# Attention with a group norm in front: the first transferred group sends 12 of its 16 squares, GpSimd copies the other four, and the homes are three

## The reference

```python
y = ((xg - mu) * rsqrt(var + EPS)).reshape(B, C, H, W) * gn_gamma + gn_beta   # 4 groups of 32 channels
q, k, v = split(einsum('bchw,dc->bdhw', y, w_qkv) + b_qkv, 3)
scores = einsum('bnc,bcm->bnm', q, k) * C ** (-0.5)
w = softmax(scores, axis=-1)
a = einsum('bnm,bmc->bnc', w, v)
out = einsum('bchw,dc->bdhw', a, w_out) + b_out
return x + out
```

## Time and profile before

| what | us |
|---|---|
| median of three runs | 137.77 |
| lowest and highest run | 137.07, 138.37 |
| profiled execution, its own time | 138.07 |
| its span, first to last instruction | 136.3 |
| PE busy | 129.4 (95% of the span) |
| DVE busy | 99.8 (73%) |
| ACT busy | 65.0 (48%) |
| POOL busy | 41.4 (30%) |

### The profile page before, as it was taken

How to read it: one execution, slowest core, us unless ns; L and a number is a source line. 1 busy time by engine, 2 the same in 40 slices (tenths; PEclk the granted TensorE clock), 3 DMA queues, 4 the chain that set the end, 5 groups by cost and what they waited for, 6 DMA issues and landing times.

```text
span 136.3 us, 1759 instructions
## 1 busy us (share of the span) xinstructions
PE 129.4 (95%) x543; PEld 89.1 (65%) x543; DVE 99.8 (73%) x170; ACT 65.0 (48%) x117; POOL 41.4 (30%) x49
## 2 busy tenths in 40 slices
PE   6999999998999949999999999999999999999990
PEld 6987688875777526666666666666656577554670
DVE  0589699999998996877686889866868886761302
ACT  3154778854675372544542475544633474730000
POOL 6032130730022229300190058000770367303210
PEclk9999999999999999999999999999999999999999
DMA  4940000030056978985689656888888459961011
GB/s 152 350 191 0 0 5 0 3 77 0 0 111 147 210 188 236 207 203 169 154 204 206 204 114 160 191 195 224 203 202 201 122 123 209 209 176 77 0 77 77
DMA packets 8937, 19.01 MB, mean 139 GB/s; under 512 B 3040, under 2 KB 3040, under 8 KB 8928
## 3 DMA queue, kind: packets, MB, share of 16 engines
q1 hardware_dynamic: 8640, 18.63, 53.8%
q10 hardware_dynamic: 288, 0.27, 0.6%
HBM read 4.20 MB, written 2.11 MB: 46 GB/s over the span
## 4 chain that ended last, share of the span: by engine, by line
PE 75%; DVE 12%; SPq 7%; issue 2%; DMA 2%; DVEq 0%
PE mixed L833 31%; PE scores L778 7%; SPq L255 7%; PE scores L779 7%; PE scores L781 7%; DVE scores L577 5%; PE scores L839 4%; PE turned L798 3%; DVE flipped_odd L605 3%; PE turned L723 3%; DMA home_odd<-flipped_odd 2%; PE mixed L830 1%; PE mixed L828 1%; PE mixed L829 1%; PE mixed L723 1%
## 5 line engine op out<-in xcount | busy, mean ns | idle before, releaser
L577 DVE TENSOR_SCALAR_CACHE_REDUCE scores<-scores,key_bias 128x1024 f32<-128x1024 f32 x31 | 40.0, 1289 | 15.0 <-PE scores L781 14.7
L426 ACT ACTIVATE probs<-scores,neg_max 128x1024 f32<-128x1024 f32 x32 | 35.7, 1116 | 22.7 <-DVE scores L577 21.9
L833 PE MATMUL mixed<-home_odd,v 128*128 128x512 f32 x48 | 22.6, 594 | 1.9 <-DMA home_odd<-flipped_odd 1.9
L833 PE MATMUL mixed<-home_even,v 128*128 128x512 f32 x48 | 22.1, 594 | 0.0
L778 PE MATMUL scores<-y_hi_odd,z_hi_odd 128*128 128x512 f32 x32 | 18.7, 585 | 0.6 <-DVE z_lo_odd L544 0.6
L778 PE MATMUL scores<-y_hi_even,z_hi_even 128*128 128x512 f32 x30 | 15.9, 531 | 0.0
L605 DVE STREAM_TRANSPOSE flipped_odd<-probs 128x1024 f32<-128x1024 f32 x12 | 14.8, 1235 | 0.3 <-DMA home_odd<-flipped_odd 0.3
L605 DVE STREAM_TRANSPOSE flipped_even<-probs 128x1024 f32<-128x1024 f32 x12 | 14.8, 1234 | 0.0
L833 PEld LDWEIGHTS mixed<-home_even,v 128*128 128x128 f32 x48 | 8.9, 189 | 7.8 <-issue 7.2
L833 PEld LDWEIGHTS mixed<-home_odd,v 128*128 128x128 f32 x48 | 8.5, 190 | 8.3 <-issue 8.0
L779 PE MATMUL scores<-y_lo_odd,z_hi_odd 128*128 128x512 f32 x32 | 12.6, 392 | 0.0
(11 more groups left out here) (162 smaller groups left out, 202.9 us busy)
## 6 DMA issues: line engine op xcount, KB each, us to landing
home_odd<-flipped_odd SPq DMA_DIRECT2D x48, 128.0 KB, 2.4
home_even<-flipped_even SPq DMA_DIRECT2D x48, 128.0 KB, 2.4
out_dram<-result SPq DMA_DIRECT2D x8, 256.0 KB, 3.5
inv_wide<-inverse_rows SPq DMA_DIRECT2D x7, 256.0 KB, 3.6
xs<-in_x_dram SPq DMA_DIRECT2D x2, 512.0 KB, 6.5
xs<-in_x_dram SPq DMA_DIRECT2D x3, 256.0 KB, 4.6
xs<-in_x_dram ACTq DMA_DIRECT2D x1, 256.0 KB, 3.3
ws<-in_weights_dram SPq DMA_DIRECT2D x1, 256.0 KB, 4.0
```

Source lines behind the costliest of these rows:

```text
L426: act.activation(probs[:, i % RING, :], scores[:, i % 2, :], ACT.Exp, bias=neg_max[:, i:i + 1], scale=-1.0, accum_out=row_sum[:, i:i + 1]) ...
L577: dve.tensor_scalar(scores[:, i % 2, :], scores[:, i % 2, :], key_bias[:, b % 2, i:i + 1], None, ALU.subtract, ALU.min, accum_out=neg_max[ ...
L833: mm = pe.matmul(bank, v[:, b % 2, k, :], there, start=first, stop=final)
```

## The change

Three things. `swap` leaves out k = 0 for group 1, so that it issues 12 squares in place of 16 (`squares_sent`), and the semaphore counts of `swaps` follow. POOL copies the four diagonal squares of group 1 instead (`diagonal`), two after block 7's z tail and two in block 8, each behind the one before; PE's first tile of group 1 waits for all four as well as for the transfers, and so do the flips of group 3, which overwrite the buffer. And there are three homes by the group's number modulo 3 in place of two by its parity. The room for the third is that of `first_turned`: `home_0` has the same place in memory, group 3 is the first to use it, and a swap now waits for the mixed tiles of the group three before.

```diff
+    HOMES = 3
...
-        first_turned = sb("first_turned", [128, KT, HALF])
...
-        home = sb("home_even", [128, GROUP]), sb("home_odd", [128, GROUP])
+        with nc.sbuf_tensor("first_turned", [128, KT, HALF], fp32) as first_turned:
+            pass
+        home_0 = sb("home_0", [128, GROUP])
+        home = home_0, sb("home_1", [128, GROUP]), sb("home_2", [128, GROUP])
...
+        def squares_sent(group):
+
+            return SQ * (SQ - 1) if group == SWAPPED[0] else SQ * SQ
+
         def swaps(group):
 
-            return SWAP * len([g for g in SWAPPED if g <= group and g % 2 == group % 2])
+            return sum(16 * squares_sent(g) for g in SWAPPED if g <= group and g % HOMES == group % HOMES)
...
                 sp.wait_ge(s_flipped, QB * group)
-                if group > 2:
-                    sp.wait_ge(s_mixed, KT * (group - 1))
-                for k in range(SQ):
+                if group >= HOMES:
+                    sp.wait_ge(s_mixed, KT * (group - HOMES + 1))
+                for k in range(1 if group == SWAPPED[0] else 0, SQ):
...
+            def diagonal(g):
+                pool.wait_ge(s_flipped, QB)
+                if g == 0:
+                    pool.wait_ge(s_z_lo, HALVES)
+                else:
+                    pool.wait_ge(s_diagonal, g)
+                if g == 2:
+                    pool.wait_ge(s_rstd, 3)
+                pool.tensor_scalar(home[1][32 * g:32 * g + 32, g * N:(g + 1) * N], flipped[1][32 * g:32 * g + 32, g * N:(g + 1) * N],
+                                   1.0, None, ALU.mult).then_inc(s_diagonal, 1)
...
                     if i == 7 and b + 1 < BATCHES:
                         z_tail(b + 1)
+                    if n in (7, 8):
+                        diagonal(2 * (n - 7))
+                        diagonal(2 * (n - 7) + 1)
+                        pool.wait_ge(s_diagonal, 2 * (n - 6))
...
                 dve.wait_ge(s_exp, n + 1)
+                if group == 3:
+                    dve.wait_ge(s_diagonal, SQ)
                 if group > 2:
-                    dve.wait_ge(s_swapped[group % 2], swaps(group - 2))
+                    dve.wait_ge(s_swapped[(group - 2) % HOMES], swaps(group - 2))
...
                         if group in SWAPPED:
-                            pe.wait_ge(s_swapped[g], swaps(group))
+                            pe.wait_ge(s_swapped[group % HOMES], swaps(group))
+                            if group == SWAPPED[0]:
+                                pe.wait_ge(s_diagonal, SQ)
```

More of the change, by code:

```diff
@@ L47, in attention_kernel @@
     PAIRS = KT // 2
-    SWAP = 16 * SQ * SQ
+    HOMES = 3
     MIX = {4: [(0, 1)], 5: [(0, 1)], 6: [(0, 1)], 7: [(0, 1)], 8: [(0, 1)], 9: [(0, 1)], 10: [(0, 2)]}
@@ L189, in attention_kernel @@
         s_flipped = sem("squares_flipped")
-        s_swapped = [sem("squares_swapped_even"), sem("squares_swapped_odd")]
+        s_diagonal = sem("first_diagonal_squares_copied")
+        s_swapped = [sem(f"squares_swapped_{k}") for k in range(HOMES)]
         s_mixed = sem("mixed_tiles_done")
@@ L249, in swap @@
                 sp.wait_ge(s_flipped, QB * group)
-                if group > 2:
-                    sp.wait_ge(s_mixed, KT * (group - 1))
-                for k in range(SQ):
+                if group >= HOMES:
+                    sp.wait_ge(s_mixed, KT * (group - HOMES + 1))
+                for k in range(1 if group == SWAPPED[0] else 0, SQ):
                     for g in (0, 2, 1, 3):
                         t = g ^ k
-                        sp.dma_start(home[group % 2][32 * t:32 * t + 32, g * N:(g + 1) * N],
+                        sp.dma_start(home[group % HOMES][32 * t:32 * t + 32, g * N:(g + 1) * N],
                                      flipped[group % 2][32 * g:32 * g + 32, t * N:(t + 1) * N]
-                                     ).then_inc(s_swapped[group % 2], 16)
+                                     ).then_inc(s_swapped[group % HOMES], 16)
             def store(group):
@@ L433, in turned_copy @@
                     return
-                act.wait_ge(s_swapped[1], swaps(5))
+                act.wait_ge(s_swapped[5 % HOMES], swaps(5))
                 for j in range(2):
@@ L831, in mix @@
                     else:
-                        there = home[g][:, :].rearrange("p (g v u c) -> p v u g c", g=SQ, v=KT, u=QB)[:, k, :, :, :]
+                        there = home[group % HOMES][:, :].rearrange("p (g v u c) -> p v u g c", g=SQ, v=KT, u=QB)[:, k, :, :, :]
                         mm = pe.matmul(bank, v[:, b % 2, k, :], there, start=first, stop=final)
```

## The result

| | median, us | profiled execution, us | its span, us | mean clock of PE |
|---|---|---|---|---|
| before | 137.55 (137.07 to 138.37) | 138.07 | 136.3 | 0.999 |
| after | 143.34 (142.29 to 143.38) | 143.35 | 141.5 | 0.974 |

The ratio is 1.040, with a 95% interval of 1.033 to 1.047. The prediction said 136.0, with a range of 135.3 to 137.3.

The account below looks back on a forecast made before the run. PE was taken as the bound, busy 95% of the span, with one hole that matters. Closing it gave -1.85 us, the other terms 0: 136.22 from the profiled execution, 135.92 from the median; forecast 136.0, range 135.3 to 137.3.

Parts of the forecast that it names:

- Twelve issues close the hole of 1.85 us: Before group 1's first mixed tile: PE's idle wait for squares, ended by late SyncE issues, closes whole; 1.85 us gained.
- first rival: The hole before group 1's mixed tiles is smaller in most executions: gain 0.82 us, time 136.95; chance 0.25.
- The copies take 1.12 us each: Four GpSimd copies of group 1's diagonal squares, priced by a one-input 128x1024 row; bounds 0.72 and 2.39 us.
- upper bound of 2.39: Highest price considered for one GpSimd copy, in us, from a two-input operation of 128x1024.
- Copies home at 47.70, PE's wait at 49.15: GpSimd's queue ends the fourth copy at 47.70, before transfers (48.31) and PE (49.15); costs the path nothing.
- The rival of slow copies: At group 1's first mixed tile and the projection behind: slow copies hold PE, about 140.4 at 2.39 us each; chance 0.07.
- The smallest margin is y's tail at the projection: The next image's y, queued behind the copies, is ready at 51.74; PE's projection needs it at 52.33, 0.6 to spare.
- The port lock: GpSimd copies hold VectorE's two norm_b operations through shared SBUF ports, DVE 1.12 us late; still 136.0; chance 0.03.
- The third home gives nothing: Group 3's transfers waited last for their own flips (64.52), so releasing a home earlier gains 0.0 us.
- DVE behind the hole catches up: VectorE, following an earlier PE, takes up scores 0.56 us late at most, once; its idle time absorbs this.
- Group 6's margin of 0.2 us stays: Group 6's last square lands at 120.18, PE takes its first at 120.36; both move by 1.85 us.

Follow-up runs that it names:

- the fast copies: The changed kernel with a second operation (multiply by 1.0 twice) in its four GpSimd copies; 136.03 us, ratio to before 0.989.

## Why the prediction was wrong

- *Twelve issues close the hole of 1.85 us.* Right. With the copies out of the way the hole is closed, and the gain is 1.57 us in the median, between the two sizes of the hole that the forecast and its first rival named.
- *The copies take 1.12 us each.* **This step failed**, and it is the cause. It rested on "instruction kind and row length are the same". They weren't: the row of 1.12 us has two operations in one instruction, like every one-input row and the 0.72 one in the earlier trace rows, and the copy has one. The doubt was put on the 32 partitions, which turned out to cost nothing. A copy measured 2.77 us, above the upper bound of 2.39 as well, since the bound was taken from a two-input operation and not from the copy's own form. The trace of before had one row of this form, the last constant that POOL makes:

```profile
2.99 0.54 POOL L294 TENSOR_SCALAR minus_mean<-group_mean 128x128 f32<-128x128 f32 x1
```

  0.54 us for 128 elements beside 0.72 for 384 should have raised the question; it lies on the measured line of the slow form, 0.2 + 128 x 2.5 ns.
- *Copies home at 47.70, PE's wait at 49.15.* With 2.77 us each, the same sum gives 41.32 + 4 x 2.77 + 0.70 + 5 x 0.24 = 54.3; measured 53.68, because the five steps between operations took 0.75 us in all rather than 1.2, and the z tail ended at 41.14 rather than 41.32. The arithmetic of the queue was right, and with two operations the copies end at 46.61.
- *The rival of slow copies* had the place and the side, but 0.07 of the chance, and it priced only the waits: about 140.4 at 2.39 us. Its own rule, 0.4 us for each 0.1 us per copy from 1.28 on, gives 142.0 at the measured 2.77, and 143.34 was measured. What it lacked is PE's clock. Behind the hole of 4.86 us PE worked at the lower level for about 5 us, and that is 1.7 of the 5.8 us lost.
- *The smallest margin is y's tail at the projection.* Right place, wrong sign: 0.6 us to spare forecast, a wait of 0.3 measured with the fast copies. Of the 0.9 between them, 0.5 comes from norm_a, held next to the fourth copy; 0.3 is the step from the end of the tail's first half (50.62 + 1.29 = 51.91) to PE's start (52.17), which the margin left out; 0.1 is a PE that came sooner.
- *The port lock* had the small operations behind the root as its place, and the delay is there, but it fell on norm_a and not on the two norm_b operations that the prediction named. It made DVE's maximum 0.5 us late and not 1.12, and what followed for PE is the wait for y's tail, not one for group 2's squares.
- *The third home gives nothing*: no gain was found, and a cost of up to 0.7% isn't excluded. *DVE behind the hole catches up*: right, PE has no wait for it in the kernels without a hole.
- *Group 6's margin of 0.2 us stays.* Nearly: with the copies left out there was a wait of 0.2, with the fast copies none.
- The time of 136.0 us that was forecast is that of the kernel whose copies have the form that was priced: 136.03. That it fits to the decimal is partly luck: that kernel gained 1.4 us on a kernel before of 137.41 in its own series, where the sum took 1.85 from 137.77.

## What to carry to other kernels

Price an added instruction by a row of exactly its form: the operations that it chains count as much as its shape, and a row that differs in one of them is no price and not even a safe bound: the 2.39 us taken as the upper one lay below the 2.77 measured. Where an operation on GpSimd has no second operation, try it with a neutral one, or as a plain copy; in this kernel the neutral operation was worth 7.3 us. And where a bound would open a hole of several microseconds in front of PE, add what the lower clock behind it costs, here 1.7 us.

## What the runs showed of the hardware

- On GpSimd, `tensor_scalar` without a second operation took 2.76 to 2.85 us for 1024 fp32 elements per partition, with one 1.03 to 1.20, a plain copy 1.03 to 1.04, a two-input addition of a tile to itself 1.88. The slow form took the same on 32, 64 and 128 partitions, two operations and the copy the same on 32 and 128.
- PE's granted clock stayed at 1.00 behind 1.85 us of idle time, and was 0.50 from 53 to 59 us behind 4.86 us of it. Matmuls on zeros in the hole, with gaps of 0.28 and 0.42 us, kept it at 1.00.
- Most issues of the same 128 KB transfer took 0.5 to 0.6 us, on SyncE's queue and on ScalarE's, but single ones up to 2.1 on SyncE's and 1.43 on ScalarE's. Landing took 2.4 us (median) with SyncE issuing alone, and 3.6 to 3.8 from both queues while both issued, at 233 GB/s.
